# Chunk 1's third group of pair products moves into step 0, and layer 2's low weight parts move ahead of it

## The chip, the cores and the metric

One core of one Trainium2 chip. The time is the device time of one launch in microseconds (us). The engines are TensorE (PE in the profile, with its weight loads as PEld), VectorE (DVE), ScalarE (ACT), GpSimd (POOL) and SyncE (SP, which here only issues DMAs).

## The reference, cut to what matters

```python
e = stack([tbl_f[ids[:, f]] for f in range(39)], axis=1)      # 512 x 39 x 16
prev = e
for k in range(3):                                            # widths 39, 128, 128 -> 128
    z = einsum('bmd,bhd->bdmh', e, prev).reshape(b, 16, 39 * h)
    t = transpose(z @ w[k] + b[k])                            # 512 x 128 x 16
    t = t / sqrt(sum(t * t over the last two axes))
    logit.append(t); prev = t
feat = concat([sum(concat(logit, axis=1), axis=-1), dense_ctx], axis=1)   # 512 x 400
y = relu(relu(feat @ W_top1 + b) @ W_top2 + b) @ W_top3
```

## The kernel before

The batch is cut into 16 chunks of 32 examples, so that a chunk has 512 columns (example, element). x of a chunk is gathered by 10 indirect DMAs of GpSimd, stored to a DRAM scratch, and read back by SyncE in several layouts: `x_pairs` (rotations of the fields, three semaphores `pairs_loaded[p]`) and `x_sq`, which `turn_x` transposes into the columns `x_col` that are used as scalars.

**Layer 0** uses the symmetry of the product: VectorE makes the products of pairs of fields in `make_pairs(c, p)` for four groups p (tiles 0 and 1, 2 and 3, 4 and 5, and tile 6, which is made of squares), and TensorE sums them with `pair_matmul(c, tile)` into `acc0`.

**Layers 1 and 2** are a list of jobs, `JOBS`, also called steps: step n is one (layer, chunk, quarter of 128 columns). Steps 0 to 3 are layer 1 of chunk 0, steps 4 to 7 layer 1 of chunk 1, steps 8 to 11 layer 2 of chunk 0, and so on, 128 steps. In a step TensorE multiplies a quarter of `prev` with the weights of all 39 fields; a bank holds four fields. Values and weights are split into a high and a low part (`prev_hi`, `prev_lo`, `w_hi`, `w_lo`), so a bank costs three matmuls, lines 735 to 737. Five banks of a step (A banks, ring of 2) are scaled by ScalarE (L572) and added by GpSimd (L450); five (D banks, ring of 3) are scaled and added by VectorE, one instruction a field (`add_field`, L963), and `merge` (L982) joins the sums. The first four `add_field` of a step wait for GpSimd's four adds of that step. TensorE runs seven A banks ahead (`LEAD`): ahead of step 0 it does the A banks 0 to 6 alone, and then, in each step, places 0 to 9 in turn D bank, A bank, D bank, ... A turned sum of each step (L778) goes to `turned`, from which ScalarE and VectorE finish the layer (`finish_squares`, `sum_squares`, `norms`, `roots`, `reciprocal_step`, `finish_values`, `sum_values`, `make_prev`, `high`, `low`).

**Order.** The order on each engine is written out: each engine walks over (step n, place, A bank a, or field u) and looks up what else is to be done there in tables (`PAIRS_AT`, `PAIR_MATMULS_AT`, `TURNS_AT`, `GATHERS_AT`, `W2_HIGH_AT`, `W2_LOW_AT`, `FINISHES`, `NORMS`). Before step 0 stands a start written out by hand: gathers, weights of layer 1 split, products of chunk 0, its layer 0, its norm, and `prev` of chunk 0 in two pieces. Then VectorE makes all four groups of chunk 1 (L1080) before its first `add_field`, and TensorE sums the seven tiles in step 0, at the places of `PAIR_MATMULS_AT`.

**Weights of layer 2.** They are loaded in three parts (fields 0 to 13, 14 to 26, 27 to 38; 896, 832 and 768 KB) and split in six pieces. ScalarE rounds a piece to its high part (`split_high`, L553), then VectorE subtracts (`split_low`, L905). The first two pieces are split ahead of step 0 (the low parts at L1052, ahead of `sum_squares(0, 0)`), the others in steps 1 to 4. Layer 2 begins in step 8, and its A banks in step 6. The weights of layer 1 are needed from the first bank.

Of the kernel before, what the change touches and what calls it, by code (L numbers as in the profile page):

```python
# [32 lines left out]
NP = len(PAIR_GROUPS)  # L33
# [86 lines left out]


PAIRS_AT, SQUARES_AT, PAIR_MATMULS_AT = {}, {}, {}
for _c in range(1, CHUNKS):
    _it = _c - 1
    if _it == 0:

        _made = []
        _summed = {(0, 0): [0, 1], (0, 2): [2, 3], (0, 4): [4, 5], (0, 6): [6]}
    else:
        _i = [step_at(_it, q) for q in range(3)]  # L130
        if _it == 1:
            _made = [(_i[0], 2), (_i[0], 12), (_i[1], 8), (_i[2], 2)]
            _summed = {(_i[0], 5): [0], (_i[0], 8): [1]}
        else:
            _last = step_at(_it - 1, 7)
            _made = [(_last, 4), (_i[0], 12), (_i[1], 8), (_i[2], 2)]
            _summed = {(_last, 8): [0], (_i[0], 2): [1]}
        _summed.update({(_i[0], 9): [2], (_i[1], 4): [3], (_i[1], 9): [4], (_i[2], 2): [5], (_i[2], 8): [6]})
    if _it:
        SQUARES_AT[step_at(_it, 1), 3] = _c  # L140
    PAIRS_AT.update({at: (_c, p) for p, at in enumerate(_made)})
    PAIR_MATMULS_AT.update({at: (_c, tiles) for at, tiles in _summed.items()})


# [6 lines left out]
W_LOADS = {1: [(0, 16), (16, 28), (28, 39)], 2: [(0, 14), (14, 27), (27, 39)]}  # L151
W_PIECES = {1: [(0, 16), (16, 28), (28, 39)], 2: [(0, 7), (7, 14), (14, 21), (21, 27), (27, 33), (33, 39)]}

GATHERS_BEFORE = 7


GATHERS_AT = {(0, 1 + j - GATHERS_BEFORE): (2, j) for j in range(GATHERS_BEFORE, GATHERS)}
# [6 lines left out]

W2_LOADS_FIRST, W2_FIRST = 1, 2
W2_HIGH_AT = {(1, 1): 2, (1, 2): 3, (2, 1): 4, (2, 2): 5}
W2_LOW_AT = {(1, 14): 2, (2, 10): 3, (3, 10): 4, (4, 8): 5}


CTX_ROWS = 2 * 32 + EMB
# [8 lines left out]
def cin_kernel(nc, idx_in, base_in, table, ctx_t, w0a, w0b, w1, w2, b0, b1, b2,  # L181
# [7 lines left out]
    with ExitStack() as ctx:  # L189
# [182 lines left out]
        def load_partners(queue, c, p):  # L372

            tiles = [i for i in PAIR_GROUPS[p] if c or i >= PICKED]
            if tiles:
                for kk in range(PER_TILE):
                    load_rows(queue, c, p, x_rot[kk * FIELDS:(kk + 1) * FIELDS, tiles[0]:tiles[0] + len(tiles), :],
                              PAIR_OFFSETS[PER_TILE * tiles[0] + kk], [[ROWS, FIELDS], [PER_TILE * ROWS, len(tiles)]])
            if p < 2:
                tile, _, *partners = EXTRA_PAIRS[p]  # L380
                for i, partner in enumerate(partners):
                    if tile + i in tiles:
                        load_rows(queue, c, p, x_rot[PAIR_ROWS:128, tile + i, :], partner, [[2 * ROWS, EXTRA]])
# [113 lines left out]
        @block.sync  # L497
        def _(sp):
            def store_chunk(c):
                g = gathered[:, c % 2, :, :]  # L500
                dst = scratch[c, :, :]
                full = (GATHERS - 1) * 128
                sp.wait_ge(gather_done[c % 2], gathered_by(c))
                sp.dma_start(dst[0:full, :].rearrange("(j p) e -> p j e", p=128),
                             g[:, 0:GATHERS - 1, :]).then_inc(scratch_stored, 16)
                sp.dma_start(dst[full:full + LAST_SLOTS, :].rearrange("(j p) e -> p j e", p=LAST_SLOTS),
                             g[0:LAST_SLOTS, GATHERS - 1:GATHERS, :]).then_inc(scratch_stored, 16)
                sp.dma_start(dst[FIELDS * CB:SCRATCH_FIELDS * CB, :].rearrange("(j p) e -> p j e", p=128),
                             g[:, 0:5, :]).then_inc(scratch_stored, 16)

            sp.dma_start(ids_sb[:, :], idx_in).then_inc(ids_loaded, 16)
            sp.dma_start(base_sb[:, :], base_in).then_inc(ids_loaded, 16)
            store_chunk(0)
            for c in range(CHUNKS):
                sp.wait_ge(scratch_stored, (c + 1) * 48)
                if c:
                    sp.wait_ge(pairs_made, c * NP)
                for p in range(NP - 1):
                    if p < 2:
                        load_reps(sp, c, p)  # L520
                    if c:
                        load_partners(sp, c, p)
                if c:
                    sp.wait_ge(x_col_made, c)
                load_squares(sp, c)
                if c == 1:
                    for part in range(W2_LOADS_FIRST, len(W_LOADS[2])):
                        load_raw(sp, 2, part)
                if c == 4:

                    sp.wait_ge(w_lo_made[1], len(W_PIECES[1]))
                    sp.wait_ge(w_lo_made[2], len(W_PIECES[2]))
                    sp.wait_ge(ctx_cleared, 1)
                    for row in range(0, CTX_ROWS, 32):
                        sp.dma_start(top1c_raw[row:row + EMB, :],
                                     w_top1[3 * 128:3 * 128 + EMB, :]).then_inc(top_loaded, 16)
                        sp.dma_start(ctx_raw[row:row + EMB, :], ctx_t).then_inc(top_loaded, 16)
                    sp.dma_start(top1_sb, w_top1[0:3 * 128, :].rearrange("(k p) n -> p k n", p=128)
                                 ).then_inc(top_loaded, 16)
                    sp.dma_start(top2_sb, w_top2.rearrange("(k p) n -> p k n", p=128)).then_inc(top_loaded, 16)  # L540
                if c + 1 < CHUNKS:
                    store_chunk(c + 1)
            sp.wait_ge(y_done, 1)
            sp.dma_start(out, y_sb[:, :]).then_inc(y_stored, 16)
            sp.wait_ge(y_stored, 16)

        @block.scalar
        def _(act):
# [27 lines left out]
            def square_x(c):  # L576
                act.wait_ge(pairs_loaded[0], pairs_landed(c, 0))
                if c:

                    act.wait_ge(pairs_made, c * NP)  # L580
                    act.wait_ge(pairs_summed, c)
                nc.scalar.activation(z0[0:PAIR_ROWS, SQUARES, :], x_rep[0:PAIR_ROWS, :],
                                     ACT.Square).then_inc(x_squared, 1)
                act.wait_ge(x_squared, c + 1)
                nc.scalar.activation(z0s[:, :], z0[0:PAIR_ROWS, SQUARES, :], ACT.Copy).then_inc(squares_hi_made, 1)
# [4 lines left out]
            def finish_squares(k, c):  # L590
                f = FINISH_NO[k, c]
                if k == 0:
                    act.wait_ge(pairs_summed, c + 1)
                else:
                    act.wait_ge(turn_done, JOB_AT[k, c, TILES - 1] + 1)
                if f:
                    act.wait_ge(squares_summed, f)
                nc.scalar.activation(squares[:, :], layer_sums(k)[:, :], ACT.Square,
                                     bias=bias[:, k:k + 1]).then_inc(squared, 1)
# [68 lines left out]
                split_high(2, piece)  # L668
            for p in range(1, NP - 1):
                load_partners(act, 0, p)  # L670
            act.wait_ge(bias_loaded, 48)
            square_x(0)
            finish_squares(0, 0)
            finish_values(0, 0)
            roots(0)
# [51 lines left out]
        def _(pe):  # L727
# [11 lines left out]
            def bank_for_act(at):  # L739
                n, a = divmod(at, A_BANKS)  # L740
                if n >= NJ:
                    return
                k, c, q = JOBS[n]
                if n == 0:
                    m = a * PER_BANK
                    pe.wait_ge(w_lo_made[1], 1 + sum(m >= lo for lo, _ in W_PIECES[1][1:]))
                if (k, c, q) == (2, 0, 0) and a == 0:
                    pe.wait_ge(w_lo_made[2], len(W_PIECES[2]))
                if n == 0 and a == 0:
                    pe.wait_ge(prev_first_lo_made, 1)  # L750
                elif a == 0 and q == (1 if (k, c) == (1, 0) else 0):
                    pe.wait_ge(prev_lo_made[k], c + 1)
                if at >= A_RING:
                    pe.wait_ge(a_scaled, at - A_RING + 1)
                three_terms(bank_a[at % A_RING], k, c, q, a * PER_BANK, a_fields_of(a)).then_inc(a_ready, 1)
# [79 lines left out]
            keep_busy(2)  # L835
            for at in range(LEAD):
                bank_for_act(at)
            N1, N2 = TOP1 // 128, TOP2 // 128
            tops = [acc0, bank_a[0], bank_a[1], bank_d[0]]
            feats = [(top1c_sb, ctx_sb[:, :])] + \  # L840
# [60 lines left out]
        def _(dve):  # L901
# [146 lines left out]
                split_low(1, piece)  # L1048
            for p in range(NP):
                make_pairs(0, p)  # L1050
            turn_x(0)
            for piece in range(W2_FIRST):  # L1052
                split_low(2, piece)
            sum_squares(0, 0)
            for step in range(R_STEPS):
                reciprocal_step(0, step)

# [19 lines left out]
            first_low(slice(COLS, ROWS), prev_lo_made[1])  # L1077
            sum_values(0, 0)
            features(0)
            for p in range(NP):  # L1080
                make_pairs(1, p)

            def clear_ctx():
# [123 lines left out]
```

## Time and profile before

| what | us |
|---|---|
| median of three runs | 1050.79 |
| the three runs | 1050.82, 1050.79, 1046.94 |
| profiled execution, its own time | 1049.29 |
| its span, first to last instruction | 1047.5 |
| TensorE busy | 1019.5 (97%) |
| VectorE busy | 967.0 (92%) |
| GpSimd busy | 872.4 (83%) |
| ScalarE busy | 795.6 (76%) |

The granted TensorE clock is 1.000 of full speed over the span. Times in the rows are from the start of the span. In a row of a timeline the number in front is the start, the next the duration, and the brackets hold the idle time of that engine before the row and what released it. The first bank of layer 1 starts at 42.95, and step 0 begins with the D bank at 50.59.

### The profile page before, as it was taken

What the parts mean: (1) busy time and instruction counts of PE and PEld (TensorE: products, weight loads), DVE (VectorE), ACT (ScalarE), POOL (GpSimd) and SP (SyncE); (2) the same over time, 40 slices, a digit from 0 to 9 for tenths busy, and PEclk for the clock granted to TensorE, in tenths of its full rate; (3) what the DMA queues carried; (4) which work ended last, traced back from release to release, by engine and by line L of the source; (5) the groups of instructions that cost most, each with busy time, mean ns of one, the idle gap of its engine ahead of it and who ended that gap; (6) DMA issues with size and microseconds to landing.
All of it is one profiled execution on the core that took longest, in us unless ns stands there. A gap on an engine that the chain in (4) does not pass through costs nothing.

```text
span 1047.5 us, 17976 instructions
## 1 busy us (share of the span) xinstructions
PE 1019.5 (97%) x4322; PEld 786.8 (75%) x4322; DVE 967.0 (92%) x3345; ACT 795.6 (76%) x2655; POOL 872.4 (83%) x729
## 2 busy tenths in 40 slices
PE   2999999999999999999999999999999999999998
PEld 0467777878777787877778787777878777787883
DVE  2589999999999999999999999999999999999993
ACT  3476878878787887878788787878878787888872
POOL 6778989898888989888898989889898887777770
DMA  5540030412103030210303021030302103000000
GB/s 189 132 138 19 4 89 3 97 53 57 36 6 87 3 90 3 49 45 5 88 3 90 2 56 37 4 89 3 90 2 50 42 4 88 1 1 1 2 1 1
DMA packets 75892, 46.10 MB, mean 44 GB/s; under 512 B 55689, under 2 KB 58633, under 8 KB 75658
## 3 DMA queue, kind: packets, MB, share of 16 engines
q1 hardware_dynamic: 68487, 38.59, 15.5%
q10 hardware_dynamic: 2179, 5.07, 1.4%
q0 software_dynamic: 5120, 1.29, 1.4%
q8 instruction: 34, 0.56, 0.2%
q14 instruction: 72, 0.59, 0.2%
HBM read 42.99 MB, written 1.94 MB: 43 GB/s over the span
## 4 chain that ended last, share of the span: by engine, by line
PE 94%; DVE 3%; POOL 1%; issue 1%; DMA 1%; ACT 0%; SPq 0%; DVEq 0%; ACTq 0%
PE bank_d L735 14%; PE bank_d L737 14%; PE bank_d L736 14%; PE bank_a L735 13%; PE bank_a L737 13%; PE bank_a L736 13%; PE acc L795 8%; DVE sums L963 1%; PE turned L778 1%; PE turned L816 1%; POOL gathered L433 1%; PE bank_d L890 1%; PE bank_a L845 1%; PE small L804 0%; DMA base_sb<-in_bases 0%
## 5 line engine op out<-in xcount | busy, mean ns | idle before, releaser
L450 POOL TENSOR_TENSOR sums<-sums,scaled 128x512 f32<-128x512 f32 (+1 forms) x512 | 660.7, 1291 | 113.9 <-ACT scaled L572 79.1
L963 DVE SCALAR_TENSOR_TENSOR sums<-bank_d,x_col,sums 128x128 f32<-128x128 f32 x2304 | 656.5, 339 | 32.5 <-PE bank_d L737 22.4
L572 ACT ACTIVATE scaled<-bank_a,x_col 128x128 f32<-128x128 f32 x1920 | 555.7, 385 | 134.0 <-PE bank_a L737 125.6
L735 PE MATMUL bank_d<-w_hi,prev_lo 128*128 128x512 f32 x640 | 279.0, 436 | 2.2 <-DVE sums L982 2.0
L735 PE MATMUL bank_a<-w_hi,prev_lo 128*128 128x512 f32 (+1 forms) x640 | 269.4, 421 | 2.5 <-issue 1.7
L737 PE MATMUL bank_d<-w_hi,prev_hi 128*128 128x512 f32 x640 | 252.6, 395 | 0.0
L736 PE MATMUL bank_d<-w_lo,prev_hi 128*128 128x512 f32 x640 | 252.4, 394 | 0.0
L737 PE MATMUL bank_a<-w_hi,prev_hi 128*128 128x512 f32 (+1 forms) x640 | 245.4, 383 | 0.0
L736 PE MATMUL bank_a<-w_lo,prev_hi 128*128 128x512 f32 (+1 forms) x640 | 244.8, 383 | 0.0
L572 ACT ACTIVATE sums<-bank_a,x_col 128x128 f32<-128x128 f32 x512 | 146.6, 370 | 65.1 <-PE bank_a L737 64.2
L433 POOL DMA_INDIRECT gathered<-in_table,idx x160 | 168.8, 1055 | 28.2 <-issue 14.7
L735 PEld LDWEIGHTS bank_a<-w_hi,prev_lo 128*128 128x128 f32 x640 | 120.5, 188 | 47.2 <-issue 15.6
L736 PEld LDWEIGHTS bank_a<-w_lo,prev_hi 128*128 128x128 f32 x640 | 120.6, 188 | 38.7 <-issue 13.9
L735 PEld LDWEIGHTS bank_d<-w_hi,prev_lo 128*128 128x128 f32 x640 | 120.6, 188 | 38.2 <-DVE sums L963 9.1
L737 PEld LDWEIGHTS bank_d<-w_hi,prev_hi 128*128 128x128 f32 x640 | 120.4, 188 | 28.3
L736 PEld LDWEIGHTS bank_d<-w_lo,prev_hi 128*128 128x128 f32 x640 | 121.1, 189 | 26.8 <-issue 7.2
L737 PEld LDWEIGHTS bank_a<-w_hi,prev_hi 128*128 128x128 f32 x640 | 120.2, 188 | 22.4
L795 PE MATMUL acc<-z,w_sb 128*128 128x512 f32 (+1 forms) x192 | 96.8, 592 | 0.3 <-DVE z L931 0.3
L963 DVE SCALAR_TENSOR_TENSOR bank_d<-bank_d,x_col,sums 128x128 f32<-128x128 f32 x256 | 78.8, 348 | 0.0
L931 DVE TENSOR_TENSOR z<-x_pairs 128x1024 f32<-128x1024 f32 (+1 forms) x46 | 72.2, 1570 | 4.1 <-DMA x_pairs<-x_scratch 2.8
L982 DVE TENSOR_TENSOR sums<-bank_d,sums 128x128 f32<-128x128 f32 x256 | 71.3, 278 | 0.0
L795 PEld LDWEIGHTS acc<-z,w_sb 128*128 128x128 f32 (+1 forms) x192 | 36.0, 189 | 12.4 <-issue 4.8
(85 smaller groups left out, 537.7 us busy)
## 6 DMA issues: line engine op xcount, KB each, us to landing
x_pairs<-x_scratch SPq DMA_DIRECT2D x135, 156.0 KB
x_pairs<-x_scratch SPq DMA_DIRECT2D x96, 78.0 KB
gathered<-in_table,idx POOLq DMA_INDIRECT x160
x_sq<-x_scratch SPq DMA_DIRECT2D x32, 64.0 KB
x_pairs<-x_scratch SPq DMA_DIRECT2D x92, 22.0 KB
x_scratch<-gathered SPq DMA_DIRECT2D x16, 72.0 KB
w_raw<-in_w ACTq DMA_DIRECT2D x1, 1024.0 KB, 5.2
w_raw<-in_w ACTq DMA_DIRECT2D x1, 896.0 KB
```

What stands on the lines that cost most here:

```text
L433: nc.gpsimd.indirect_dma_start(out=gathered[0:n, c % 2, j, :], out_offset=None, in_=table[:, :], in_offset=bass.IndirectOffsetOnAxis(ap=id ...
L450: nc.gpsimd.tensor_tensor(out=sums[:, n % SUMS, 0:w, :], in0=sums[:, n % SUMS, 0:w, :], in1=scaled[:, a - 1, 0:w, :], op=ALU.add).then_inc ...
L572: op = nc.scalar.activation(to[:, i, :], bank_a[at % A_RING][:, i * UNITS:(i + 1) * UNITS], ACT.Copy, scale=x_of(c, q, a * PER_BANK + i))
L735: nc.tensor.matmul(to, lo, w_h, start=True, stop=False)
L736: nc.tensor.matmul(to, hi, w_l, start=False, stop=False)
L737: return nc.tensor.matmul(to, hi, w_h, start=False, stop=True)
L778: nc.tensor.transpose(turned[:, q * COLS:(q + 1) * COLS], sums[:, n % SUMS, TOTAL, :], identity[:, :]).then_inc(turn_done, 1)
L795: nc.tensor.matmul(acc0[:, :], w0_sb[0:rows, tile, :], z0[0:rows, tile, :], start=(tile == 0), stop=False)
L816: nc.tensor.matmul(turned[:, :], ones[:, :], w_raw[1][:, 0:4, :].rearrange("p m u -> p (m u)"), start=True, stop=True)
L931: nc.vector.tensor_tensor(out=z0[0:rows, tiles[0]:tiles[0] + count, :], in0=x_reps[min(p, 1)][0:rows, :].unsqueeze(1).to_broadcast([rows, ...
L963: nc.vector.scalar_tensor_tensor(out=taken(n, u) if u in LEFT else total, in0=taken(n, u), scalar=x_of(c, q, A_FIELDS + u), in1=total, op0 ...
L982: nc.vector.tensor_tensor(out=out, in0=in0, in1=in1, op=ALU.add).then_inc(merged, 1)
```

## The change

Group 2 (tiles 4 and 5) and the squares (group 3) of chunk 1 are no longer made ahead of step 0 but behind fields 3 and 7 of step 0. Tiles 0 and 1 are summed behind lead banks 5 and 6, the others one at a time in step 0. Part 1 of layer 2's weights is loaded by ScalarE's queue behind chunk 0's partners (before: by SyncE's queue behind the loads of chunk 1), and pieces 2 and 3 get their high parts between `square_x(0)` and `finish_squares(0, 0)`. The low parts of pieces 0 and 1 no longer stand ahead of `sum_squares(0, 0)` but ahead of chunk 1's group 0; that of piece 2 ahead of group 1. `turn_x(0)` goes behind `sum_squares(0, 0)`. The low part of piece 4 moves from step 3 to step 4, that of piece 5 from step 4 to step 5. One of chunk 2's gathers moves from the start into step 0.

```diff
+LEAD_TILES = {5: [0], 6: [1]}
...
-        _made = []
-        _summed = {(0, 0): [0, 1], (0, 2): [2, 3], (0, 4): [4, 5], (0, 6): [6]}
+        _made = [None, None, (0, 3), (0, 7)]
+        _summed = {(0, 0): [2], (0, 1): [3], (0, 3): [4], (0, 4): [5], (0, 6): [6]}
...
-    PAIRS_AT.update({at: (_c, p) for p, at in enumerate(_made)})
+    PAIRS_AT.update({at: (_c, p) for p, at in enumerate(_made) if at})
...
-GATHERS_BEFORE = 7
+GATHERS_BEFORE = 6
...
-W2_LOADS_FIRST, W2_FIRST = 1, 2
-W2_HIGH_AT = {(1, 1): 2, (1, 2): 3, (2, 1): 4, (2, 2): 5}
-W2_LOW_AT = {(1, 14): 2, (2, 10): 3, (3, 10): 4, (4, 8): 5}
+W2_LOADS_FIRST, W2_LOADS_SECOND = 1, 2
+W2_FIRST, W2_SECOND = 2, 4
+W2_HIGH_AT = {(2, 1): 4, (2, 2): 5}
+W2_LOW_AHEAD = [[0, 1], [2]]
+W2_LOW_AT = {(2, 10): 3, (4, 8): 4, (5, 8): 5}
... (SyncE)
-                    for part in range(W2_LOADS_FIRST, len(W_LOADS[2])):
+                    for part in range(W2_LOADS_SECOND, len(W_LOADS[2])):
                         load_raw(sp, 2, part)
... (ScalarE)
                 load_partners(act, 0, p)
+            for part in range(W2_LOADS_FIRST, W2_LOADS_SECOND):
+                load_raw(act, 2, part)
             act.wait_ge(bias_loaded, 48)
             square_x(0)
+            for piece in range(W2_FIRST, W2_SECOND):
+                split_high(2, piece)
             finish_squares(0, 0)
... (TensorE)
             for at in range(LEAD):
                 bank_for_act(at)
+                for tile in LEAD_TILES.get(at, []):
+                    pair_matmul(1, tile)
... (VectorE)
+            sum_squares(0, 0)
             turn_x(0)
-            for piece in range(W2_FIRST):
-                split_low(2, piece)
-            sum_squares(0, 0)
...
-            for p in range(NP):
+            for p, pieces in enumerate(W2_LOW_AHEAD):
+                for piece in pieces:
+                    split_low(2, piece)
                 make_pairs(1, p)
```

## Rows read from the trace of the kernel before

**Rows 1.** Busy time of each engine in stretches (start:end, length, then the engines)

```profile
43.00:51.00 8.00, 6.13 (x23) 3.95 (x24) 3.72 (x5) 6.38 (x24) 6.04 (x6) 1.00 0.77 195
51.00:60.50 9.50, 9.50 (x33) 5.87 (x33) 7.84 (x15) 5.20 (x18) 7.14 (x6) 1.00 0.56 186
60.50:91.00 30.50, 28.90 (x126) 21.97 (x124) 29.29 (x99) 25.70 (x85) 24.48 (x20) 1.00 0.34 77
91.00:147.00 56.00, 56.00 (x240) 43.48 (x241) 55.09 (x194) 43.68 (x147) 50.36 (x43) 1.00 0.20 44
203.00:1020.00 817.00, 816.79 (x3552) 646.84 (x3552) 789.75 (x2781) 651.65 (x2205) 702.48 (x577) 1.00 0.16 36
```

**Rows 2.** Timeline of TensorE, the last waits of the lead, and tiles 0 and 1 in step 0

```profile
49.07 0.47 PE L735 MATMUL bank_a<-w_hi,prev_lo 128*128 128x512 f32 x1 [0.27 <-ACT scaled L572]
...
51.28 1.88 PE L795 MATMUL acc<-z,w_sb 128*128 128x512 f32 x4
```

**Rows 3.** Timeline of VectorE, from the first norm into step 0

```profile
39.35 0.69 DVE L990 TENSOR_REDUCE ssq<-squares 128x32 f32<-128x512 f32 x1 [0.61 <-ACT squares L598]
40.77 0.35 DVE L1000 RECIPROCAL r_first<-root 128x32 f32<-128x32 f32 x1 [0.73 <-issue]
...
45.79 1.23 DVE L931 TENSOR_TENSOR z<-x_pairs 128x1024 f32<-128x1024 f32 x1 [1.15 <-issue]
...
49.85 2.24 DVE L931 TENSOR_TENSOR z<-x_pairs 128x1024 f32<-128x1024 f32 x1 [2.83 <-DMA x_pairs<-x_scratch]
...
53.95 1.77 DVE L915 SCALAR_TENSOR_TENSOR z0s<-z0s,low_rows,z 117x512 fp32r<-117x512 f32 x1
...
60.66 0.35 DVE L963 SCALAR_TENSOR_TENSOR sums<-bank_d,x_col,sums 128x128 f32<-128x128 f32 x1 [1.81 <-PE bank_d L737]
...
63.35 0.69 DVE L990 TENSOR_REDUCE ssq<-squares 128x32 f32<-128x512 f32 x1 [0.71 <-ACT squares L598]
```

**Rows 4.** Timeline of GpSimd, the adds beside these products, and step 1

```profile
46.48 1.67 POOL L450 TENSOR_TENSOR sums<-sums,scaled 128x512 f32<-128x512 f32 x1 [1.49 <-issue]
...
49.72 1.28 POOL L450 TENSOR_TENSOR sums<-sums,scaled 128x512 f32<-128x512 f32 x1
...
51.15 1.79 POOL L450 TENSOR_TENSOR sums<-sums,scaled 128x384 f32<-128x384 f32 x1
...
71.15 2.03 POOL L455 TENSOR_TENSOR prev_lo<-prev,prev_hi 128x512 fp32r<-128x512 f32 x1 [0.99 <-ACT prev_hi L622]
```

**Rows 5.** ScalarE and its queue ahead of layer 0's finish of chunk 0

```profile
23.78 3.00 ACTq L364 DMA_DIRECT2D x_pairs<-x_scratch  x7
...
38.63 0.69 ACT L598 ACTIVATE squares<-acc,bias 128x512 f32<-128x512 f32 x1 [7.44 <-issue]
```

**Rows 6.** Instructions on the raw weights to 100 us (ns min/median/max), and their transfers

```profile
L553 ACT ACTIVATE w_hi<-w_raw x9: 866/950/1892, 12.2 to 76.6; 128x896 fp32r<-128x896 f32 x3, 128x768 fp32r<-128x768 f32 x3, 128x2048 fp32r<-128x2048 f32 x1, 128x1536 fp32r<-128x1536 f32 x1
L905 DVE TENSOR_TENSOR w_lo<-w_raw,w_hi x9: 942/1101/2292, 20.7 to 92.3; 128x896 fp32r<-128x896 f32 x3, 128x768 fp32r<-128x768 f32 x3, 128x2048 fp32r<-128x2048 f32 x1, 128x1536 fp32r<-128x1536 f32 x1
...
DMA to landing us min/median/max: 5.2/5.4/6.1
```

**Rows 7.** The page's group of the gathers (busy, mean ns, idle before)

```profile
L433 POOL DMA_INDIRECT gathered<-in_table,idx x160 | 168.8, 1055 | 28.2 <-issue 14.7
```

**Rows 8.** Timeline of TensorE, its later stalls in steps 1 to 4

```profile
72.35 0.50 PE L735 MATMUL bank_d<-w_hi,prev_lo 128*128 128x512 f32 x1 [0.25 <-DVE sums L963]
...
74.24 0.50 PE L735 MATMUL bank_d<-w_hi,prev_lo 128*128 128x512 f32 x1 [0.21 <-DVE sums L982]
...
89.09 0.50 PE L735 MATMUL bank_d<-w_hi,prev_lo 128*128 128x512 f32 x1 [0.55 <-DVE sums L982]
...
90.95 1.10 PE L795 MATMUL acc<-z,w_sb 128*128 128x512 f32 x2 [0.26 <-DVE z L931]
```

**Rows 9.** Timelines of VectorE and TensorE around step 6's fourth D bank

```profile
109.65 0.85 DVE L963 SCALAR_TENSOR_TENSOR sums<-bank_d,x_col,sums 128x128 f32<-128x128 f32 x3
...
110.17 0.48 PE L735 MATMUL bank_d<-w_hi,prev_lo 128*128 128x512 f32 x1
```

## The prediction

> **What bounds the kernel now.** I read the busy time by stretch first, then the timeline of TensorE for its idle time, then what VectorE, GpSimd and ScalarE do at those places.
>
> TensorE bounds the kernel: from 203 to 1020 us it is busy 816.79 of 817.00 us, and from 91 to 147 us all 56.00 [rows 1]. Its work stays the same in the change (the same banks and the same seven tiles), so the time can move only by TensorE's idle time. The change touches nothing behind step 5, so that is its idle time up to about 100 us: the wait for chunk 0's x and `prev` up to 42.95, then 1.87 us in 43 to 51 (the lead), none in 51 to 60.5, and 30.50 - 28.90 = 1.60 us in 60.5 to 91 [rows 1]. These last 3.5 us, a third of a per cent, are all that could be won behind the first bank.
>
> The lead is paced by ScalarE: its last wait, 0.27 us ahead of bank 5 at 49.07, ends with a scaled bank [rows 2]. In the third stretch the stalls end with VectorE: 0.25, 0.21, 0.55 and 0.26 us, together 1.27 us, at 72.35, 74.24, 89.09 and 90.95 [rows 8]; the other 0.33 of the 1.60 lies ahead of them. VectorE is busy 29.29 of 30.50 us there and 55.09 of 56.00 in the next stretch [rows 1]: it runs behind, not far.
>
> **The change, part by part.**
>
> *Ahead of the first norm.* Two low parts leave the time ahead of `sum_squares(0, 0)`. They cost 1.0 us each, but VectorE waited there for ScalarE's squares anyway (0.61 us of idle time is left even behind them) [rows 3, 6]: no gain. `turn_x(0)`, at most some 0.5 us as a copy of 256 columns against 0.69 us for a reduction of 512, now stands between 39.35 + 0.69 = 40.04 and the reciprocal at 40.77, where VectorE idles 0.73 us [rows 3]: no loss. Were that cover gone, it would cost its 0.5 us.
>
> *Two high parts on ScalarE, and their load.* ScalarE idles 7.44 us ahead of 38.63 [rows 5]. Two high parts of 896 and 768 columns cost 0.95 and 0.87 us [rows 6], so they must start by 38.63 - 1.82 = 36.8. Their load is issued behind seven transfers that end at 26.8 [rows 5]; this load took 5.4 to 6.1 us from issue to landing from SyncE [rows 6], so it lands at 33 if nothing is in its way. It isn't alone: chunk 0's x layouts, the gathers and `x_sq` are under way. The slack of 3.8 us makes it 0 in the sum; the bound on the other side is a rival below. Nothing else waits on ScalarE then but `square_x(0)`, which stands ahead. In steps 1 and 2 ScalarE is 1.8 us lighter, but none of the stalls at 72.35 to 90.95 ends with ScalarE [rows 8]: 0.
>
> *Tiles 0 and 1 in the lead.* They stand behind bank 5, and from there to 60.5 TensorE has no idle time to fill [rows 1, 2]; all its waits in the lead lie ahead of bank 5. So the two tiles delay bank 6 and the D bank of place 0 by their own 1.88 us [rows 2] and give it back in step 0: 0 for TensorE. What they need is group 0, made by 47.02 before [rows 3].
>
> *The low parts ahead of groups 0 and 1.* VectorE is free from 45.79 - 1.15 = 44.64, and idles 1.15 and 2.83 us ahead of groups 0 and 1 [rows 3]: 3.98 us of room for three low parts of 1.0 us, about what fits. But GpSimd adds lead banks at the same time, and rows 3 and 4 show the two engines taking turns. Group 0 takes 1.23 us, group 1 2.24 us for the same shape: it starts at 49.85, while GpSimd's add of 49.72 runs to 51.00. The next add, of only 384 columns, takes 1.79 us where one of 512 took 1.28; it starts at 51.15, while group 1 runs to 52.09. So I lay them out in turns, with some 1.2 us an add, 1.1 us a product and 1.0 us a low part: low parts to 46.6, add 1 (asked for at 46.48 [rows 4]) to 47.8, group 0 to 48.9, add 2 to 50.1, low part 2 to 51.1, add 3 to 52.3, group 1 to 53.4, add 4 to 54.3. Tile 2 is wanted two tiles later than the first tile before, at 51.28 + 1.88 = 53.1 [rows 2]. It would wait **0.3 us**. Without turns group 1 would end at 51.1: 0. With every turn at its full row (1.28 and 1.23), group 1 ends near 54.2: 1.1 us. The value taken is nearest to the rows with overlaps.
>
> The Trainium skill (SBUF — State Buffer, section "Who interferes with whom") states it as a lock: a VectorE instruction with two SBUF inputs and a GpSimd instruction that reads SBUF exclude each other, the second waits for the whole first. The trace agrees: 51.00 + 1.09 = 52.09. By that rule the low parts, with two SBUF inputs, are the wrong work for this place, and the wait is 0.3 us; without it, it would be 0.
>
> *Group 2 and the squares in step 0.* The first `add_field` waits for add 4, so it starts at 54.3 instead of 55.64 (53.95 + 1.77, less the overlap) [rows 3]. Four fields of 0.27 us, group 2 in 1.2 to 2.2 us, four fields, squares in 0.7 to 1.8 us [rows 3]: group 2 is ready by 56.7 to 57.6, tile 4 is wanted at about 57.3; the squares by 59.5, tile 6 is wanted at about 60.7. Before, VectorE idled 1.81 us ahead of 60.66, and again 0.71 us ahead of 63.35 [rows 3], which takes up what is late: 0. So VectorE gets to field 12 no earlier than before, since it waits there for TensorE.
>
> *One gather moved.* It takes 1.06 us [rows 7] out of the start, where GpSimd idles 1.49 us before its first add, and goes into step 0, just ahead of step 1's adds. The next cover is the 0.99 us ahead of `prev_lo` at 71.15 [rows 4]. Chunk 2's store and loads on SyncE go some 2.4 us later; their first product, ahead of 90.95, is not awaited. 0.
>
> *Low parts in steps 1 to 5.* The part of step 1 (1.0 us) is gone, ahead of 72.35; that of step 3 goes into step 4, and that of step 4 into step 5. VectorE is 1.0 us earlier at 72.35 and 2.0 us at 89.09, more than the stalls there: **-1.27 us** [rows 6, 8]. From step 5 on it is only 1.0 us lighter than before, less what it then waits for TensorE itself (some 0.4 us, since in step 5 it would otherwise be 0.7 us ahead of its banks), and the part in step 5 may take a turn with an add (0 to 0.5 us). In step 6 VectorE frees the ring at 109.65 + 0.34 = 109.99, and TensorE takes it at 110.17 [rows 9]: 0.18 us of slack. TensorE can stay ahead by 0.5 + 0.18 there, and no more; **+0.6 us** comes back (0 to 1.3).
>
> **Sum.** 0.3 - 1.27 + 0.6 = -0.4 us: the span goes from 1047.5 to 1047.1, the profiled execution's time from 1049.29 to 1048.9. The median of the runs lies 1.5 us above that execution, so the forecast is 1050.79 - 0.4 = 1050.4. The edits' own bounds are -1.3 and +2.4 (1.1 in step 0, all of 1.27 back).
>
> **Rivals.**
> - *The full gain.* Group 1 comes in time and step 5 hides its low part: -1.27, 1049.5. For it: the rest of the trace hides VectorE's work in step 5 (55.09 of 56.00 is not all). Against it: 0.18 us of slack in step 6.
> - *Turns in step 0 cost more.* Tiles 2 and 4 wait for groups 1 and 2 by 1.1 and 0.5 us, and all is given back later: +1.6, 1052.4. For it: five two-input instructions against four adds. Against it: products and low parts that run alone take 1.0 to 1.2.
> - *The load of part 1 lands late* (slower). From 36.8 on each us of lateness is one us of ScalarE ahead of chunk 0's squares, and so of the end; beyond 0.5% it decides from 42.1 on. Landing at 38.5 gives +1.7, 1052.5. For it: the transfers in flight, and x that TensorE waits for. Against it: 10 us from issue for what took 6.1 at most.
> - *Nothing changes*, because VectorE still meets TensorE at field 12 and the four stalls come back elsewhere: 1050.8.
>
> The skill's page DMA: Bandwidth & Descriptors ("Issuing engines are not separate DMA queues") says that transfers of all queues share 16 engines and interleave, so the other queue buys no bandwidth; no row here prices it, and by it the third rival gains.
>
> **How the numbers follow.** Forecast 0.42, full gain 0.15, turns 0.18, late load 0.12, nothing 0.13. 0.5% is 5.25 us, about what a measurement of this kernel can tell from no change: the three runs alone lie 3.9 us apart. Only a landing past 42.1 (0.03 of the 0.12) or scatter reaches it on the slow side, and on the fast side there are only 3.5 us to win, so scatter alone. Range: from the full gain less the runs' scatter, 1046.94 - 1.3 and rounded in as both are seldom together, 1046.2, to the late load, 1052.5. Faster 0.04, same 0.91, slower 0.05.
>
> **What would show it.** Right: TensorE idle 1.9 us in the lead as before, a stall of some tenths at tile 2, no stalls at 72 to 91, a new one of tenths in steps 6 to 9; the first `add_field` at about 54.3; the high parts of pieces 2 and 3 over by 37. Wrong: `finish_squares(0, 0)` later than 38.63, TensorE waiting for group 2 or the squares, GpSimd's adds of step 3 late by the gather.

## The result and the profile after

The changed kernel is slower by 0.28%: the ratio of its runs to those of the kernel before is 1.0028, 95% interval 1.0019 to 1.0037, with medians of 1050.61 us (1048.47 to 1054.64) and 1047.04 us (1046.12 to 1050.82) over 20 runs each. The forecast was 0.4 us faster. That its 1050.4 us lies beside the measured 1050.61 is no merit of it: it was built on the median of three early runs of the kernel before, 1050.79, of which two turned out to be the highest of the 20.

A part of the runs shows a mean granted clock of 0.995 to 0.998 and is 0.7 to 5.7 us longer, so the differences in us below are between medians of the runs at 1.000 on one chip. For the changed kernel, run again beside the experiments on another chip, that is 1049.36 - 1047.43 = +1.9 us; the ratio of that second measurement, 1.0006 (0.9993 to 1.0019), would by itself not tell the two kernels apart.

The profiled executions differ by only 0.4 us in span (1047.9 against 1047.5). The busy time by stretch, to be held against [rows 1] (columns as there):

```profile
43.00:51.00 8.00, 6.72 (x24) 4.20 (x25) 6.56 (x7) 6.82 (x25) 4.60 (x4) 1.00 0.76 199
51.00:60.50 9.50, 8.74 (x31) 5.31 (x30) 7.40 (x16) 4.25 (x15) 7.24 (x6) 1.00 0.43 119
60.50:91.00 30.50, 30.17 (x132) 23.42 (x131) 28.85 (x102) 25.12 (x85) 25.02 (x21) 1.00 0.34 78
91.00:147.00 56.00, 54.06 (x232) 41.57 (x231) 55.55 (x185) 42.41 (x143) 50.58 (x42) 1.00 0.20 43
203.00:1020.00 817.00, 816.76 (x3556) 647.57 (x3555) 790.07 (x2783) 650.64 (x2209) 702.16 (x578) 1.00 0.16 36
```

In the lead TensorE's idle time is 1.28 us instead of 1.87. That need not be the change's doing: with only the low parts of steps 3 and 4 moved, and the lead of before, it is 1.2 us as well (waits of 0.62, 0.30 and 0.28). In 60.5 to 91 TensorE's idle time fell from 1.60 to 0.33 us: the four stalls of [rows 8] are gone, as forecast. But 0.76 us came up in 51 to 60.5 and 1.94 us in 91 to 147, where there had been none. The rest of the program is untouched. In the timeline of TensorE the first of the new waits is the wait for tile 2, behind the first D bank:

```profile
52.22 0.40 PE L746 MATMUL bank_d<-w_hi,prev_hi 128*128 128x512 f32 x1
53.38 1.12 PE L804 MATMUL acc<-z,w_sb 128*128 128x512 f32 x2 [0.76 <-DVE z L942]
```

The timeline of VectorE there, and in steps 5 and 6:

```profile
44.62 2.08 DVE L916 TENSOR_TENSOR w_lo<-w_raw,w_hi 128x896 fp32r<-128x896 f32 x2
47.79 1.23 DVE L942 TENSOR_TENSOR z<-x_pairs 128x1024 f32<-128x1024 f32 x1 [1.08 <-DMA x_pairs<-x_scratch]
48.93 2.17 DVE L916 TENSOR_TENSOR w_lo<-w_raw,w_hi 128x896 fp32r<-128x896 f32 x1
51.20 2.12 DVE L942 TENSOR_TENSOR z<-x_pairs 128x1024 f32<-128x1024 f32 x1
54.32 1.13 DVE L974 SCALAR_TENSOR_TENSOR sums<-bank_d,x_col,sums 128x128 f32<-128x128 f32 x4 [1.00 <-POOL sums L455]
...
99.79 1.97 DVE L916 TENSOR_TENSOR w_lo<-w_raw,w_hi 128x768 fp32r<-128x768 f32 x1
101.68 2.31 DVE L942 TENSOR_TENSOR z<-x_pairs 117x1024 f32<-117x1024 f32 x1
...
109.29 2.04 DVE L926 SCALAR_TENSOR_TENSOR z0s<-z0s,low_rows,z 117x512 fp32r<-117x512 f32 x1
```

There are three things to see. The first `add_field` starts at 54.32, where 54.3 was forecast, and waits for GpSimd. Group 0 now waits for x until 47.79, 2.0 us later than before, and group 1 starts 1.35 us later [rows 3], right behind low part 2. In step 5 a low part that costs 0.94 us alone takes 1.97, and the product behind it 2.31.

SyncE's queue shows that x is late (start, duration):

```profile
27.36 6.59 SPq L395 DMA_DIRECT2D x_sq<-x_scratch  x2
37.30 0.39 SPq L509 DMA_DIRECT2D x_scratch<-gathered  x1
...
40.30 8.93 SPq L369 DMA_DIRECT2D x_pairs<-x_scratch  x21
```

Before, these three began at 26.94 (lasting 5.32), 36.01 and 39.01. The longer issue of `x_sq` is not what holds up the store: it ends at 33.95, and the store goes out at 37.30. The store waits for chunk 1's gathers to land (the profile names that wait in twelve of the seventeen kernels, 2.5 to 4.9 us long, and no other in the rest), and the last of them is issued at the same time in the changed kernel and in the kernel before:

```profile
33.69 0.92 POOL L438 DMA_INDIRECT gathered<-in_table,idx  x1 [0.30 <-issue]
33.74 0.92 POOL L433 DMA_INDIRECT gathered<-in_table,idx  x1 [0.30 <-issue]
```

From the end of that issue to the store pass 2.69 us, against 1.35 before. The load of part 1 is under way beside the gathers. By stretch, the last two columns are the busy share of the DMA engines and GB/s. The share is 0.99 to 1.01 from 27 to 33 in the changed kernel:

```profile
29.00:31.00 2.00, 2.00 (x6) 0.81 (x6) 0.00 (x0) 1.22 (x2) 1.70 (x3) 1.00 1.01 243
31.00:33.00 2.00, 2.00 (x6) 0.92 (x5) 1.24 (x2) 0.00 (x0) 1.50 (x2) 1.00 1.00 227
33.00:35.00 2.00, 2.00 (x6) 0.93 (x5) 1.76 (x4) 0.00 (x0) 1.39 (x3) 1.00 0.61 193
```

In the kernel before the same three read:

```profile
29.00:31.00 2.00, 2.00 (x6) 0.86 (x5) 0.00 (x0) 1.07 (x2) 1.76 (x3) 1.00 0.84 187
31.00:33.00 2.00, 2.00 (x6) 0.85 (x5) 1.30 (x2) 0.19 (x1) 1.46 (x2) 1.00 0.45 69
33.00:35.00 2.00, 2.00 (x6) 0.95 (x5) 1.76 (x4) 0.00 (x0) 1.39 (x3) 1.00 0.28 43
```

### The profile page after: what moved, and what is told of

Same layout as the page of the kernel before. It is cut to its first block, busy times and chain, and to the rows that moved or that the text cites. A ratio compares the mean times of both kernels' runs of the same rounds, so it can differ in the third digit from the quotient of the medians.

```text
span 1047.9 us, 17976 instructions
## 1 busy us (share of the span) xinstructions
PE 1019.0 (97%) x4322; PEld 787.0 (75%) x4322; DVE 968.4 (92%) x3345; ACT 793.7 (76%) x2655; POOL 871.6 (83%) x729
## 3 DMA queue, kind: packets, MB, share of 16 engines
HBM read 42.99 MB, written 1.94 MB: 43 GB/s over the span
## 4 chain that ended last, share of the span: by engine, by line
PE 89%; DVE 5%; SPq 2%; issue 1%; DMA 1%; POOL 1%; ACT 0%; DVEq 0%; ACTq 0%
PE bank_d L744 14%; PE bank_d L746 13%; PE bank_d L745 13%; PE bank_a L744 13%; PE bank_a L746 13%; PE bank_a L745 13%; PE acc L804 7%; DVE sums L974 3%; PE turned L787 1%; SPq L369 1%; POOL gathered L438 1%; PE bank_d L901 1%; SPq L395 1%; PE bank_a L856 1%; DVE z L942 1%
## 5 line engine op out<-in xcount | busy, mean ns | idle before, releaser
L745 PEld LDWEIGHTS bank_a<-w_lo,prev_hi 128*128 128x128 f32 x640 | 120.5, 188 | 38.8 <-issue 13.9
```

The source lines that it names most:

```text
L745: nc.tensor.matmul(to, hi, w_l, start=False, stop=False)
```

## The experiments

Fifteen kernels ran, on four chips, each timed beside the kernel before on its own chip. Ratios are to the kernel before, with their 95% interval; "us" is the difference of medians. The last two kernels of the text, meant to win, are not in the table. Where the changed kernel was the starting point (rows 1, 2, 4, 5, 9 and 10), the moved gather stays in, and group 2 and the squares are made in step 0, also with the tiles late. In the other rows the gather is where it was, and "early tiles" stands for the tiles with group 2 and the squares in step 0.

The expectations name their theories by letters. A: the early load costs time by itself. A2: it does so only through the transpose of chunk 0. B: the low part in step 5 costs it. C: the early tiles alone do. D: low part 2 ahead of group 1 does. AC: load and early tiles together do. E: early tiles with low parts 0 and 1 do. A stall is a stretch in which TensorE waits.

| run | early load | early tiles | low parts ahead of groups 0, 1 | low part in step 5 | ratio | us |
|---|---|---|---|---|---|---|
| changed kernel again | yes | yes | 0, 1 and 2 | yes | 1.0006 (0.9993 to 1.0019) | +1.9 |
| late load | no | yes | 0, 1 | yes | 1.0017 (1.0008 to 1.0026) | +1.6 |
| only load | yes, transpose ahead | no | none | no | 1.0008 (0.9999 to 1.0017) | +1.0 |
| lows in 3 and 4 | yes | yes | 0, 1 and 2 | no | 1.0009 (1.0000 to 1.0018) | +1.0 |
| tiles late | yes | no | 0, 1 and 2 | yes | 1.0008 (0.9999 to 1.0017) | +0.8 |
| load, transpose behind | yes | no | none | no | 0.9993 (0.9981 to 1.0005) | 0.0 |
| only tiles | no | yes | none | no | 0.9992 (0.9980 to 1.0004) | +0.1 |
| only low part in 5 | no | no | none | yes | 1.0011 (0.9997 to 1.0024) | +1.3 |
| low part 2 back | yes | yes | 0, 1 | no | 1.0001 (0.9991 to 1.0012) | +1.0 |
| both taken back | yes | no | 0, 1 and 2 | no | 0.9991 (0.9981 to 1.0000) | -0.1 |
| tiles and load | yes | yes | none | no | 1.0017 (1.0008 to 1.0025) | +1.5 |
| tiles and low parts | no | yes | 0, 1 | no | 1.0008 (0.9999 to 1.0017) | +0.4 |
| low part behind field 12 | no | no | none | yes, later | 1.0012 (1.0003 to 1.0021) | +1.2 |

Many intervals touch 1, so what follows rests on the pattern of the table together with the stalls in the profiles, not on single ratios. The differences of medians come from 10 to 12 runs (8 for the low part alone), and drawing anew from these runs moves them by 0.2 to 1.4 us either way; the ratios take in all runs, which is why a row can have a larger difference and a smaller ratio.

**First four: which part costs.** Late load (pieces 2 and 3 in steps 1 and 2 again, so low part 2 no longer stands ahead of group 1 either):

```diff
-W2_LOADS_FIRST, W2_LOADS_SECOND = 1, 2
-W2_FIRST, W2_SECOND = 2, 4
...
+W2_LOADS_FIRST, W2_LOADS_SECOND = 1, 1
+W2_FIRST, W2_SECOND = 2, 2
...
+W2_LOW_AHEAD = [[0, 1], []]
+W2_LOW_AT = {(1, 14): 2, (2, 10): 3, (4, 8): 4, (5, 8): 5}
```

> The changed kernel, but part 1 of layer 2's weights is loaded by SyncE behind chunk 1's loads, and pieces 2 and 3 are split in steps 1 and 2, as before the change. Theory A (the early load delays what stands behind it: SyncE's issue of chunk 0's squares took 6.6 us instead of 5.3, and chunk 1's store went out at 37.3 instead of 36.0): the store is back at 36.0, chunk 1's group 1 lands at about 49.9 instead of 51.2, TensorE's wait at tile 2 shrinks from 0.76 to 0.3 us or less, and most of the 2.9 us of the median goes. Theory B (the low part in step 5 meets GpSimd's adds and the products of chunk 2): the stalls of 0.91, 0.18 and 0.85 us at 104 to 112 stay, and the time stays within 1 us of the changed kernel's.

The stalls of steps 5 and 6 stayed, as theory B has it (0.95, 0.16 and 0.87 us). Theory A's forecast for the profile fell: the wait at tile 2 was 1.35 us. In this execution TensorE's first bank started at 41.6 instead of 43.0, and group 1 waited for x until 51.20, though the load was late again (the store went out at 36.50, chunk 1's first load at 39.93). Both ends of that wait move by themselves between executions. Taking the load back won 0.3 us of the 1.9 (on another chip), which the noise covers.

Only the load, in the kernel before (cut; SyncE no longer loads part 1, and ScalarE no longer splits pieces 2 and 3 in step 1):

```diff
+            load_raw(act, 2, 1)
             act.wait_ge(bias_loaded, 48)
             square_x(0)
+            for piece in (2, 3):
+                split_high(2, piece)
```

> The kernel before, with one part of the change: part 1 of layer 2's weights is loaded early by ScalarE's queue and pieces 2 and 3 get their high parts ahead of chunk 0's squares; all else as before. Theory A: slower than before by 1 to 3 us, with chunk 1's store at about 37.3 and VectorE's first field of step 0 some 1.3 us later, at about 57. Theory B: the same as before within 0.5 us, since VectorE idles 1.8 us ahead of field 12 and TensorE wants nothing of chunk 1 until 54.4.

It cost 1.0 us, but not as theory A had it. Its timeline of VectorE shows the chunk 0 transpose waiting for `x_sq`, and behind it the two low parts and the sum of squares, 0.9 us late on the path to the first bank:

```profile
37.90 0.45 DVE L944 STREAM_TRANSPOSE x_col<-x_sq 128x256 f32<-128x256 f32 x1 [1.33 <-DMA x_sq<-x_scratch]
38.26 2.05 DVE L908 TENSOR_TENSOR w_lo<-w_raw,w_hi 128x896 fp32r<-128x896 f32 x2
40.23 0.68 DVE L993 TENSOR_REDUCE ssq<-squares 128x32 f32<-128x512 f32 x1
```

So the transpose's new place, which the prediction costed at nothing, should be what keeps the early load off that path; the run with the transpose behind, below, tests it.

Low parts 4 and 5 back in steps 3 and 4 of the changed kernel (`(3, 10): 4, (4, 8): 5`):

> The changed kernel, but the low parts of pieces 4 and 5 stand in steps 3 and 4 as before the change. Theory B: TensorE's three stalls at 104 to 112 (1.94 us) go, at most 0.6 us of stalls comes back at 88 to 91, and the time falls by 1.3 to 1.9 us. Theory A: no change, or less than 0.5 us.

The three stalls went, and 0.57 and 0.24 us came back at 89 and 91. Of +1.9 (on another chip) +1.0 was left: the time fell by 0.9 and not by 1.3 to 1.9, so theory B holds for about half of the loss. Step 0 is that of the changed kernel here, and yet TensorE waited 0.99 us for tile 0 and 0.59 us for tile 2; its first bank had started at 41.93.

Tiles at the places of before in the changed kernel (`LEAD_TILES = {}`, tiles 0 and 1 behind D bank 0, 2 and 3 two places on):

> The changed kernel, but TensorE sums chunk 1's tiles at the places of before (0 and 1 behind the first D bank, 2 and 3 two places on, 4 and 5, then 6). Third theory C (tile 2 is wanted 1.7 us too early, when group 1 hangs on a transfer whose landing varies from run to run): the stall of 0.76 us at tile 2 goes, the scatter of the runs shrinks, and the time falls by 1 to 2 us. If the transfer only moves within what VectorE can take up, theories A and B expect 0.8 us or less.

+0.8 was left, and a stall of 0.41 us at tile 2 (its group 1 still stood behind low part 2) in place of 0.76. Its three stalls in steps 5 and 6 are again 0.95, 0.18 and 0.88 us.

**Then the parts alone.** The changed kernel as yardstick:

> The changed kernel again, as a yardstick on the same chip as its neighbours, and as a second profile of it. All theories: the stalls of 0.91, 0.18 and 0.85 us at 104 to 112 return; the wait at tile 2 varies with how long after TensorE's first bank the x of chunk 1 lands (0.76 us in the first profile, 1.35 us in the run with the late load, where the first bank started 1.3 us earlier). Median 2 to 3 us above the kernel before.

Its second profile has 0.68 us at tile 2 and 0.95, 0.18 and 0.90 us in steps 5 and 6; it came out at +1.9.

The load with the transpose behind the sum of squares:

> The kernel before with the early load and the early high parts alone, as in the run with only the load, but chunk 0's transpose stands behind the sum of squares, so that late x squares hold up nothing: low parts 0 and 1, sum of squares, transpose. Theory A (the early transfer costs time by itself, through chunk 1's x): still about 1 us slower than before. Rival A2 (it cost 1.0 us only because the transpose waited for x squares until 37.8 and pushed the two low parts and the sum of squares 0.9 us back): the same as before within 0.4 us, first bank at 43.0 or earlier.

0.0 against 1.0 with the transpose ahead, and the first bank at 42.39 instead of 43.83: rival A2 holds. Chunk 1's first load still went out at 40.6, and group 1 started at 51.52 instead of 49.85, and it cost nothing.

The early tiles alone:

> The kernel before with one part of the change: group 2 and the squares in step 0, tiles 0 and 1 behind lead banks 5 and 6, the others one by one. No weights, loads or gathers moved. Theory C (tile 2 is now wanted 1.7 us earlier, before chunk 1's group 1 is there, and the x of chunk 1 comes at its own time): a stall at tile 2 of 0.5 to 1.5 us, and 0.3 to 1.5 us slower than before, since some of it fills stalls of steps 1 to 4. If tiles early are harmless without the low parts beside them: the same as before within 0.3 us.

+0.1, and no stall at tile 2: group 1 started at 49.78 and ended at 49.78 + 1.23 = 51.01, ahead of the 52.19 at which TensorE took it. Theory C alone is refuted; low part 2 was not there to take turns either.

The low parts of pieces 4 and 5 alone, in the kernel before:

```diff
-W2_LOW_AT = {(1, 14): 2, (2, 10): 3, (3, 10): 4, (4, 8): 5}
+W2_LOW_AT = {(1, 14): 2, (2, 10): 3, (4, 8): 4, (5, 8): 5}
```

> The kernel before with one part of the change: the low part of piece 4 from step 3 to step 4, that of piece 5 from step 4 to step 5. Theory B (in step 5 it takes turns with GpSimd and with the product of group 2, and costs TensorE 1.9 us, while step 3's stalls of 0.8 us go): 0.5 to 1.2 us slower than before. Rival: VectorE is as late in step 6 as before, same within 0.3 us.

+1.3: theory B. TensorE's stalls in its timeline:

```profile
102.73 1.13 PE L795 MATMUL acc<-z,w_sb 117*128 117x512 f32 x2 [0.94 <-DVE z L931]
105.60 0.50 PE L735 MATMUL bank_d<-w_hi,prev_lo 128*128 128x512 f32 x1 [0.18 <-DVE sums L963]
110.34 0.50 PE L735 MATMUL bank_d<-w_hi,prev_lo 128*128 128x512 f32 x1 [0.88 <-DVE sums L963]
```

2.00 us, less the 0.81 us of stalls at 89 and 91 that are gone, is 1.2; the time agrees, a little above the 0.5 to 1.2 expected.

**What the tiles need as a partner.** Low parts 2, 4 and 5 of the changed kernel where they were:

> The changed kernel with the low parts of pieces 2, 4 and 5 where they were (steps 1, 3 and 4), so that only those of pieces 0 and 1 stand ahead of group 0. Theory D (with step 5's low part gone, what is left of the loss is that low part 2 takes turns with GpSimd's adds right ahead of group 1, which tile 2 now waits for): the stall at tile 2 goes from 0.6 to 0.3 us or less, and the time is within 0.5 us of the kernel before, against 1.0 us with low part 2 ahead. Theory C (x of chunk 1 lands too late for tile 2 by itself): the stall stays, and so does about 1 us.

+1.0, the same as with low part 2 ahead: theory D, which wanted 0.5 or less, is not borne out by the time. The ratio, 1.0001 (0.9991 to 1.0012), is too close to 1 to say it alone. The profile can't decide: it has no stall at tile 2, because there TensorE had already waited 1.78 us for ScalarE, which started on its first bank 1.2 us late, and the profile shows no cause for that.

Both edits taken back:

> The changed kernel with both of the edits that cost most taken back: low parts 4 and 5 in steps 3 and 4, and chunk 1's tiles at the places of before. What is left is the early load, low parts 0 to 2 ahead of groups 0 and 1, group 2 and the squares in step 0, and the moved gather. If the losses are those two (1.2 and 1.0 us) and add up: the same as before within 0.3 us. If something else of the change costs: 0.5 us or more slower.

-0.1: nothing else of the change costs, with the early load still in it. Tiles and load, the transpose behind and the low parts ahead of the sum of squares:

> The kernel before with the early load (transpose behind the sum of squares, which alone changed nothing) and the early tiles with group 2 and the squares in step 0 (which alone changed nothing). Low parts 0 and 1 stay ahead of the first sum of squares, all others in steps 1 to 4. Theory AC (the early load makes chunk 1's x some 1.4 us late, and the early tiles are what makes TensorE feel it): the two together cost 0.6 to 1.1 us, with a stall at tile 2. Theory E (it is the low parts ahead of group 0 that make the early tiles cost something): the same as before within 0.3 us.

Tiles and low parts, without the load:

> The kernel before with the early tiles, group 2 and the squares in step 0, and low parts 0 and 1 ahead of chunk 1's group 0, with the transpose behind the sum of squares; no early load, low parts 2 to 5 in steps 1 to 4 as before. Theory AC: x of chunk 1 comes at its old time, so the same as before within 0.3 us. Theory E: 0.6 to 1.1 us slower, like the changed kernel with low part 2 back in step 1 (1.0 us).

+1.5 against +0.4: theory AC, though both are above what it expected (0.6 to 1.1, and 0.3 or less). Load alone 0.0, tiles alone +0.1, both +1.5. The ratio of both, at least 1.0008, lies clear of those of the load (at most 1.0005) and the tiles (at most 1.0004). Against the run without the load (1.0008, 0.9999 to 1.0017) the intervals overlap. The two runs of above that also have both and nothing in step 5 came out at +1.0, so the pair costs 1.0 to 1.5 us. With the load, group 0 of the first of the two started at 47.88, and TensorE waited for it already at tile 0:

```profile
50.11 1.10 PE L800 MATMUL acc<-z,w_sb 128*128 128x512 f32 x2 [0.65 <-DVE z L938]
```

Low part 5 behind field 12 of step 5, in the kernel before:

> The run with only the low parts of pieces 4 and 5 moved (1.3 us slower), but that of piece 5 in step 5 behind field 12 and no longer right ahead of chunk 2's product of group 2, which tile 4 waits for at field 8. If the place ahead of that product is the cause: the stall of 0.9 us at 103 goes, those of step 6 stay, and the loss shrinks to 0.4 us or less. If it is only that VectorE has no time to spare in steps 5 and 6: the loss stays at 1 us or more, with the stalls all in step 6.

+1.2, so the place ahead of tile 4's product is not the cause of the loss. The stall of 0.94 us went, and 0.45 and 1.42 us stood in step 6 instead. The timeline of VectorE shows the low part at its price alone, and the squares' product longer:

```profile
102.27 0.94 DVE L905 TENSOR_TENSOR w_lo<-w_raw,w_hi 128x768 fp32r<-128x768 f32 x1
...
107.01 2.58 DVE L915 SCALAR_TENSOR_TENSOR z0s<-z0s,low_rows,z 117x512 fp32r<-117x512 f32 x1
```

In both places that were tried, VectorE has no microsecond to spare in steps 5 and 6.

**Two versions meant to win.** Both are the kernel before with the early load, the transpose behind, tiles and products as before, and nothing new in step 5. The first makes low part 2 ahead of group 0 and low part 3 ahead of group 1 (`W2_LOW_AT = {(2, 10): 4, (4, 8): 5}`), the second low part 2 alone (`{(2, 10): 3, (3, 10): 4, (4, 8): 5}`).

> A version meant to win: the kernel before, with the early load, low parts 0 and 1 ahead of the first sum of squares, chunk 0's transpose behind it, low part 2 ahead of chunk 1's group 0 and low part 3 ahead of group 1 (where VectorE idles 1.15 and 2.83 us), low part 4 in step 2, none in steps 1 and 3, low part 5 in step 4 as before; all products and tiles as before. By theories B and D nothing new stands in step 5, and group 1 is wanted late: the stalls of 0.25, 0.21, 0.55 and 0.26 us at 72 to 91 go, 0.8 to 1.3 us faster than before. If the turns ahead of group 1 reach into step 0: 0 to 0.4 us faster.

> The same, but only low part 2 ahead of group 0, nothing between groups 0 and 1, and low parts 3, 4 and 5 in steps 2, 3 and 4 as before. The two stalls at 72 and 74 go, those at 89 and 91 stay or shrink: 0.3 to 0.6 us faster than before.

The first was to be 0.8 to 1.3 us faster and was slower: 1.0018 (1.0007 to 1.0030), +0.6 us from only five runs. All four stalls went, and one of 2.12 us came at 110.47. VectorE had come to chunk 2's squares early, into a row of GpSimd instructions. VectorE's timeline:

```profile
106.69 3.46 DVE L918 SCALAR_TENSOR_TENSOR z0s<-z0s,low_rows,z 117x512 fp32r<-117x512 f32 x1
```

and GpSimd's:

```profile
105.84 1.30 POOL L450 TENSOR_TENSOR sums<-sums,scaled 128x512 f32<-128x512 f32 x1
107.09 1.28 POOL L455 TENSOR_TENSOR prev_lo<-prev,prev_hi 128x512 fp32r<-128x512 f32 x1
108.33 2.96 POOL L450 TENSOR_TENSOR sums<-sums,scaled 128x512 f32<-128x512 f32 x2
```

The second was to be 0.3 to 0.6 us faster: 0.9997 (0.9986 to 1.0008), -0.35 us, no difference that this measurement can tell, though the two stalls at 72 and 74 went as expected. No version was shown to beat the kernel before.

## Why the prediction was wrong

- **TensorE's idle time up to 100 us is all there is to move, and the four stalls go (-1.27).** Right: 1.60 us of idle time became 0.33.
- **Low parts in steps 1 to 5, +0.6 (0 to 1.3) comes back.** This is the step that failed first. Measured alone, moving the two low parts costs a net 1.3 us, so with the 0.81 us won at 89 and 91 about 2.0 us come back, above the upper end. Right was that VectorE has 0.18 us of slack in step 6 [rows 9]. Wrong were two sizes. One is the 0.5 us by which TensorE was to stay ahead thanks to a lighter VectorE, and which no row gives. The move of low part 2 did not reach step 5: in the changed kernel the low part there starts 3.35 us before TensorE wants tile 4 (99.79, and 104.05 - 0.91), and with only low parts 4 and 5 moved 3.34 us (98.45, and 102.73 - 0.94). So the stalls are the same, 1.94 and 2.00 us. The other is the turns: a turn of "0 to 0.5 us" for the low part was 1.03 (1.97 against 0.94), and the turns of the instructions behind it were left out: the product of group 2 went from 1.77 us in the kernel before to 2.31 and the squares' product from 1.43 to 2.04. A delay of VectorE moves its later two-input instructions to other places among GpSimd's, and there they were longer. That is 1.03 + 0.54 + 0.61 on top of the low part's own 0.94; the 1.4 us by which VectorE was ahead of the kernel before where the low part starts is eaten, and 1.94 us of stalls follow.
- **Tile 2 waits 0.3 us (0 to 1.1).** In the two profiles of the changed kernel 0.76 and 0.68, inside the bounds; with only low parts 4 and 5 put back, and step 0 the same, 0.99 at tile 0 and 0.59 at tile 2, above them. The layout in turns was right in its order, and its result for the first `add_field` exact, but in part by luck: group 0 was laid out behind GpSimd's first add until 47.8, and waited for x until 47.79. The layout took the x of chunk 1 as given.
- **The early load costs 0 while it lands by 36.8.** This is the second step that failed. It was right for what was priced: the load landed in time, if 2 us later than the 33 forecast (ScalarE's high parts started at 35.03), and alone it cost 0.0. Wrong as a term of the sum, since the load was looked at only for its own landing. Others came late beside it: chunk 1's first load goes out at 40.1 to 41.1 us in the eleven profiles with it, against 38.8 to 40.1 in the six without. Alone that is hidden by tiles that are wanted late; with the early tiles it is not. The pair costs 1.0 to 1.5 us where the parts cost 0.0 and 0.1. The prediction added its terms one by one, and the zeros of load and tiles are each right alone. How much of the changed kernel's own loss is the load's is less sure: 1.3 for step 5 and 1.0 to 1.5 for the pair are more than the 1.9 measured, and with the load taken back 1.6 was left.
- **Moved transpose 0, moved gather 0, tiles in the lead 0.** The first two hold: with only the early tiles and step 5's low part taken back, the time is that of the kernel before (-0.1). The third holds only without the early load (+0.1).
- **The edits' own bounds, -1.3 and +2.4.** The upper one does not follow from its terms: 1.1 in step 0, less 1.27, plus at most 1.3 that comes back, is +1.1. The measured +1.9 lies above it.
- **The rivals.** "Turns in step 0 cost more" had the side right and the place half right. The full gain came true in steps 1 to 4 only. The rule of the Trainium skill's page DMA: Bandwidth & Descriptors ("Issuing engines are not separate DMA queues"), that all queues' transfers share 16 engines, was tied to the wrong victim, the load itself; the trace agrees with it in the DMA share of 0.99 to 1.01 from 27 to 33 us and the gathers that land later there.
- **The base.** The median of three runs was 3.75 us above that of 20. The change in us was the only part of the forecast that could be argued from the profile, and there the sign was missed: -0.4 against +1.9 (the yardstick) to +2.9 (0.28% of the 20 runs).

What stays open: the profiled spans differ by 0.4 us and the medians by 1.9 (the yardstick) to 3.6 (the 20 runs each). In all fifteen experiments the profiled execution took 0.1 to 2.6 us more than the median, and in the seventeen profiles TensorE starts its first bank between 41.6 and 45.1. With starts at 41.63, 41.93, 42.62 and 43.02, the waits at tiles 0 to 2 were 1.35, 1.58, 0.68 and 0.76 us. That suggests that a run near the median starts earlier and waits longer at the early tiles; no such run was profiled, so this is argued and not shown. Two delays of ScalarE, in profiles with the early load, are open too: its first bank 1.2 us late with low parts 2, 4 and 5 put back, and chunk 0's root 1.8 us late with both edits taken back.

## What to carry to other kernels

When a change moves a transfer earlier and a consumer earlier, cost them together: the slack that hides the one is what the other uses up. For a transfer, ask not only when it lands but which transfers stand behind it, and who is waiting for those. An instruction that shares something with another engine has no fixed price; where its engine has less than a microsecond of slack, every such instruction behind it has to be laid out anew.

## What the runs showed of the hardware

A VectorE instruction with two SBUF inputs took 0.94 us alone and up to 2.03 us beside GpSimd adds for 768 columns of a low part, and the squares' product of 512 columns took 0.74, 1.43, 2.04, 2.58 and 3.46 us. The longest had the most GpSimd instructions in a row in front of it. They don't strictly take turns. In [rows 4] they did, where GpSimd's adds are 0.15 us apart. In the first version meant to win, GpSimd had an add, a low part of `prev` and an add, of which the last two started 0.05 and 0.04 us ahead of the end of the one before, and VectorE, ready at 106.69, got its turn only behind all three. The page SBUF — State Buffer of the Trainium skill ("Who interferes with whom") has the lock, by which the second waits for the whole first; the trace agrees with the lock, and shows a wait for three.

The issue of a transfer took longer while another queue had more under way: SyncE's two issues of `x_sq` took 4.7 to 5.7 us in the six profiles without the early load and 6.4 to 8.0 us in the eleven with it, where ScalarE's queue has 832 KB more under way. The store of chunk 1, which waits for gathers, went out at 36.8 to 37.6 us in the eleven and at 35.8 to 36.8 in the six.
